# Deferring the shared units of six token tiles in a mixture-of-experts and attention kernel

## What is computed

```python
xn = _layernorm(x)
s = attn(xn)                 # layer norm with gamma, beta; q, k, v; causal softmax; o_proj; + xn
g = silu(ffn(xn))
x = x + s * g

# ffn: E = 8 experts, the 2 best of each token, and a shared part of NS = 2 units
gates = softmax(xf @ router_w.T); topv, topi = top_k(gates, 2)   # then scaled to sum 1
for e in range(8):
    routed += silu(xf @ wg[e]) * (xf @ wu[e]) @ wd[e] * g_e      # D = 512, H = 352
shared = silu(xf @ sg) * (xf @ su) @ sd                          # sg, su: 512 x 704
```

## Time and profile before

| | us |
|---|---|
| three runs | 1258.19, 1260.29, 1260.90 |
| median | 1260.29 |
| the profiled execution | 1259.98 |
| its span in the trace | 1258.2 |
| PE busy | 1176.6 (94%) |
| DVE busy | 598.5 (48%) |
| ACT busy | 456.3 (36%) |
| POOL busy | 343.9 (27%) |

### The profile page before, as it was taken

How to read it: one execution, slowest core, us unless ns; L and a number is a source line. 1 busy time by engine, 2 the same in 40 slices (tenths; PEclk the granted TensorE clock), 3 DMA queues, 4 the chain that set the end, 5 groups by cost and what they waited for, 6 DMA issues and landing times. The chain is left out here.

```text
span 1258.2 us, 21972 instructions
## 1 busy us (share of the span) xinstructions
PE 1176.6 (94%) x6958; PEld 653.6 (52%) x6959; DVE 598.5 (48%) x1198; ACT 456.3 (36%) x822; POOL 343.9 (27%) x430
## 2 busy tenths in 40 slices
PE   5899999999999559999999999997899999999996
PEld 3455555556565235555555555553444444454443
DVE  5555555555555831112112211225765776776455
ACT  4433333333332112222222222223553553554452
POOL 1030000000001431212221221212554564565653
PEclk9899999999999769999999999998999999999999
DMA  8567666766674149977777777765268368257364
GB/s 298 165 161 188 168 165 179 192 166 164 178 187 107 44 92 255 218 188 174 175 183 178 174 179 179 174 153 174 76 151 225 92 149 237 85 123 204 106 146 109
DMA packets 324802, 206.44 MB, mean 164 GB/s; under 512 B 263168, under 2 KB 271368, under 8 KB 324368
## 3 DMA queue, kind: packets, MB, share of 16 engines
q1 hardware_dynamic: 313920, 170.39, 54.1%
q0 software_dynamic: 10800, 35.40, 10.8%
q10 hardware_dynamic: 32, 0.02, 0.0%
HBM read 96.88 MB, written 45.88 MB: 113 GB/s over the span
## 5 line engine op out<-in xcount | busy, mean ns | idle before, releaser
L444 PE MATMUL pair<-arena 128*128 (+1 forms) x3240 | 509.6, 314 | 13.1 <-DMA arena<-arena 13.1
L444 PEld LDWEIGHTS pair<-arena 128*128 128x128 f16 x3240 | 316.2, 98 | 193.0 <-issue 15.0
L451 PE MATMUL bank<-arena 128*128 (+1 forms) x1215 | 289.9, 385 | 8.9 <-ACT arena L884 5.1
L451 PEld LDWEIGHTS bank<-arena 128*128 128x128 f16 x1215 | 119.9, 99 | 138.8 <-issue 13.1
L1265 DVE SCALAR_TENSOR_TENSOR arena<-pair,arena 128x352 f32<-128x352 f32 x71 | 37.2, 525 | 269.9 <-ACT arena L1237 266.1
L1517 PE MATMUL pair<-arena 128*128 128x512 f16 x672 | 154.1, 385 | 2.9 <-PEq L1122 2.9
L1237 ACT ACTIVATE arena<-pair 128x352 f32<-128x352 f32 x71 | 33.0, 464 | 214.5 <-PE pair L444 214.5
L1517 PEld LDWEIGHTS pair<-arena 128*128 128x128 f16 x672 | 66.6, 99 | 78.9 <-issue 7.4
L1545 PE MATMUL bank<-arena 128*128 128x512 f16 x432 | 98.6, 379 | 7.9 <-DMA arena<-arena 7.9
L201 POOL TENSOR_TENSOR root_seed<-var_eps,minus_half 128x1 f32<-128x1 f32 x32 | 17.6, 551 | 318.6 <-DVE var_eps L210 318.5
L1532 PE MATMUL pair<-arena 128*128 128x512 f16 (+3 forms) x576 | 98.9, 326 | 1.1 <-ACT arena L1589 1.1
(11 more groups left out here) (164 smaller groups left out, 1162.0 us busy)
## 6 DMA issues: line engine op xcount, KB each, us to landing
arena<-in_L_attn_x_dram SPq DMA_DIRECT2D x96, 256.0 KB, 3.4
slot_rows<-arena SPq DMA_DIRECT2D x71, 256.0 KB
xn_rows<-arena SPq DMA_DIRECT2D x32, 256.0 KB, 2.4
shared_rows<-arena SPq DMA_DIRECT2D x32, 256.0 KB, 2.6
arena<-shared_rows SPq DMA_DIRECT2D x32, 256.0 KB, 2.9
out_dram<-arena SPq DMA_DIRECT2D x32, 256.0 KB, 3.3
arena<-in_L_ffn_wg_dram SPq DMA_DIRECT2D x32, 176.0 KB, 3.0
arena<-in_L_ffn_wu_dram SPq DMA_DIRECT2D x32, 176.0 KB, 3.4
```

Of the source, the lines that this page charges most:

```text
L444: last = pe.matmul(bank[:, 0:H], xt[:, a, c, :], weights(c, b, col), start=(c == 0 and i == 0), stop=(c == KC - 1 and i == 2))
L451: last = pe.matmul(bank[:, :], ht[:, a, c, :], weights(c, b), start=(start and c == 0 and i == 0), stop=(stop and c == HC - 1 and i == 2))
```

## The change

- **Stage 0.** The x tiles 0 and 1 are loaded behind the second part of `qkv`, ahead of the third part and of `o_proj`. Their statistics are behind group 7, their normalisation behind group 8, their split behind group 13. The four split groups stand ahead of "product 0" of k = 2 and 3, and PE's wait ahead of "product 1" no longer takes these two in. The rest of x (`x_low`) is made by POOL instead of DVE, in stage 1 too.
- **Order of tiles in stage 1.** Tiles 5, 9, 13, 17, 21 and 25 (`DEFERRED`) are routed and stored in their turn, but their shared units come last: steps 0 to 25 take the other 26 tiles (`USUAL`), steps 26 to 31 the deferred ones. In a step whose tile number jumps by two, two tiles are prepared and routed. For a deferred tile SP transposes the rows once more, now from `xn_rows` in DRAM (`turn_late`). Three xt buffers, two banks each for y and for the logits ("two row banks").
- **Expert weights** are loaded and split in steps 0 to 23: the 24 tiles of `wd` one a step, the 32 of `wg`, `wu` over the 18 steps that prepare one tile.
- **Routing** is cut in 11 pieces, one or more per half step, from step 25, b = 0 to step 30, b = 0, each behind `h_low` or `down_low` on DVE. The multiply by the token number is no longer a POOL instruction per group: eight DVE instructions with two scalar operands (128x71) make each group's hot tile.
- **Stages 1 to 3 are one block**, no barrier between them. PE goes from `unit_in(63)`, `unit_down(61)` to slot 0, `unit_down(62)`, slot 1, `unit_down(63)`. SP asks for the transposes of slots 0 and 1 and POOL for their gathers during steps 30 and 31. Stage 1 is written out without a loop.
- **SP's queue** has, per step: the next tiles' transposes, stores and loads, `turn_late`, the h transpose of the half step before, the weight loads, the y store, the h transpose of b = 0.
- Stage 4, make_gates and the slot loop's order are as before, but for names and banks.

```diff
+        DEFERRED = (5, 9, 13, 17, 21, 25)
+        USUAL = [n for n in range(NT) if n not in DEFERRED]
+        LATE = len(USUAL)
...
-                      + [("product", 0, k) for k in range(KC // 2, KC - 1)] + [("split", 0, n) for n in range(KC)]
-                      + [("product", 0, KC - 1)] + [("product", 1, k) for k in range(KC)])
-            X_STATS, X_NORMAL, X_SPLIT = 2 * KC + 1, 3 * KC, 3 * KC + 2
+                      + [("split", 0, n) for n in range(KC)] + [("product", 0, k) for k in range(KC // 2, KC)]
+                      + [("product", 1, k) for k in range(KC)])
+            X_STATS, X_NORMAL, X_SPLIT = 2 * KC - 1, 2 * KC, 3 * KC + 1
...
-                                pe.wait_ge(lo_done, g if m == 0 else g - 1)
+                                pe.wait_ge(lo_done, g if m == 0 else g - KC // 2)
...
-        def keep_x_low(dve, t, u):
-            dve.wait_ge(x16_hi, t + 1)
-            nc.vector.tensor_tensor(x16[u][:, 1], xb[u], x16[u][:, 0], ALU.subtract).then_inc(x16_lo, 1)
+        def x_low(pool, t):
+            u = t % 2
+            pool.wait_ge(x16_hi, t + 1)
+            pool.tensor_tensor(x16[u][:, 1], xb[u], x16[u][:, 0], ALU.subtract).then_inc(x16_lo, 1)
+            pool.wait_ge(x16_lo, t + 1)
...
+            def routed_in(s):
+                return range(USUAL[s] + 1, USUAL[s + 1] + 1) if s + 1 < LATE else ()
+            def normal_in(s):
+                return routed_in(s + 1)
...
+                    def turn_late(s):
+                        d = s - LATE
+                        t = DEFERRED[d]
+                        sp.wait_ge(xn_stored[t % 2], (t // 2 + 1) * 16)
+                        sp.wait_ge(gu_done, 2 * s - 2)
+                        sp.dma_start_transpose(xt[d % 2].rearrange("p s c t -> p (s c) t"), xn_rows[t * P:(t + 1) * P, :]
+                                               ).then_inc(late_turned[d % 2], 16)
...
-                v.tensor_tensor(hot_tile[n % RING], column[:].unsqueeze(1).to_broadcast([P, TG, W]),
-                                slot_hi[:, c, tiles].unsqueeze(2).to_broadcast([P, TG, W]), ALU.is_equal
-                                ).then_inc(in_tile_ready, 1)
+                for i in range(TG):
+                    t = first + i
+                    v.tensor_scalar(hot_tile[n % RING][:, i, :], column[:], slot_hi[:, c, t:t + 1], token_mid[:, t:t + 1],
+                                    ALU.is_equal, ALU.mult).then_inc(hot_ready, 1)
...
+            ROUTING = LATE - 2
+            def routing(dve, s, b):
+                at = 2 * (s - ROUTING) + b - 1
+                if at == 1:
+                    pick_best(dve, 0)
+                elif at == 2:
+                    pick_best(dve, 1)
...
+                elif at == 11:
+                    name_experts(dve)
+                    name_tokens(dve)
+            def hot_products_in(s, b):
+                at = 2 * (s - ROUTING) + b - 1
+                return {7: (0, 1), 8: (2,), 9: (3, 4), 10: (5,), 11: (6, 7)}.get(at, ())
...
+                    router(0)
+                    for s in range(NT):
+                        for b in range(2):
+                            n = 2 * s + b
+                            if n == 2 * ROUTING + 5:
+                                ranks()
+                            if s == 0:
+                                pe.wait_ge(shared_lo, NS if b == 0 else 2 * NS)
+                            unit_in(n, b)
+                            if s > 0:
+                                if n == 2:
+                                    pe.wait_ge(shared_lo, len(splits))
+                                unit_down(n - 2, b)
+                            if b == 1:
+                                for t in routed_in(s):
+                                    router(t)
+                            for m in hot_products_in(s, b):
+                                hot_product(m)
```

More of the change, by code:

```diff
@@ L348, in _ @@
                     seed(pool, 1, 1)
+                    x_low(pool, 0)
+                    x_low(pool, 1)
                 @block.tensor
@@ L1110, in early, with over_slots @@
+            slot_y_stored = slot_rows_stored
             def early(j, n):
                 return isinstance(j, int) and j < n
-            def over_slots(eng, tile, peeled, done=0):
-                for j in range(done, peeled):
-                    tile(j, j % 2, j // 2, False)
-                with eng.Fori(peeled // 2, (T - 1) // 2) as i:
+            def over_slots(eng, tile, first):
+                with eng.Fori(first // 2, (T - 1) // 2) as i:
                     tile(2 * i, 0, i, False)
@@ L1181, in _, with router @@
                 @block.tensor
                 def _(pe):
+                    def router(t):
+                        pe.wait_ge(x_turned[t % 3], (t // 3 + 1) * 16)
+                        wait(pe, logits_kept, t - 1)
+                        for c in range(KC):
+                            for i, (a, b) in enumerate(PARTS):
+                                last = pe.matmul(logit_bank[t % 2][:, 0:E], xt[t % 3][:, a, c, :],
+                                                 rw_split[:, c, b, :],
+                                                 start=(c == 0 and i == 0), stop=(c == KC - 1 and i == 2))
+                        last.then_inc(logits_done, 1)
@@ new lines, in unit_down, with ranks @@
+                    def unit_down(n, b):
+                        t = n // 2
+                        pe.wait_ge(h_turned[b], (t + 1) * 16)
+                        if b == 0:
+                            wait(pe, y_ready, t - 1)
+                        down(pe, ht[b], lambda c, s: shared_down[:, b, c, s, :], y_bank[t % 2],
+                             b == 0, b == 1).then_inc(y_done, 1)
+                    def ranks():
+                        pe.wait_ge(picks_ready, 1)
+                        picked = both16.rearrange("p t e -> p (t e)")
+                        pe.matmul(rank_bank[:, 0:NT * E], before[:, :], picked, start=True, stop=True)
+                        pe.matmul(count_bank[:, 0:NT * E], ones16[:, :], picked, start=True, stop=True
+                                  ).then_inc(ranks_done, 1)
@@ new lines, in hot_product @@
+                    def hot_product(n):
+                        pe.wait_ge(lane_ready, n + 1)
+                        pe.wait_ge(hot_ready, (n + 1) * TG)
+                        for t in range(TG):
+                            last = pe.matmul(token_bank[:, 0:W], hot_lane[n % RING][:, t, :], hot_tile[n % RING][:, t, :],
+                                             start=(n == 0 and t == 0), stop=(n == 2 * PARTS_HOT - 1 and t == TG - 1),
+                                             skip_group_check=True)
+                        last.then_inc(hot_used, 1)
@@ L1240, in slot_tile @@
+                        act.wait_ge(slot_gu_done, j + 1)
+                        if early(j, 2):
+                            act.wait_ge(h_lo, 2 * NT - 1 + j)
+                        else:
+                            wait(act, slot_h_lo, j - 1)
+                        nc.scalar.activation(sbuf[u], g_banks[u][:, 0:H], ACT.Silu,
+                                             scale=UNIT_SCALE).then_inc(slot_silu_done, 1)
+                        slot_h_high(j, u, k)
                         if last:
```

1130 lines of the change are left out of this document (557 added, 573 removed).

## The result

The changed kernel takes **1220.24 us** (median of 4 runs, 1218.99 to 1221.0), the kernel before 1259.47 us in the same comparison (4 runs, 1258.19 to 1260.9). The ratio is 0.9682, with a 95% interval of 0.9664 to 0.9701: faster, by 39 us. The forecast was 1217 us with a range of 1211 to 1228, so sign and range held and the time came out 3.2 us above the forecast. The span of the profiled execution is 1219.3 us where the sum had 1215.0: 4.3 us to explain.

A forecast was written before the change was run, and what follows sets the result against it. PE was taken to bound the kernel, with gains only where its busy share dips. Span 1258.2 - 37.2 - 7.4 + 0.7 + 0.7 = 1215.0 us, giving a forecast of 1217 us, range 1211 to 1228.

The forecast's parts named there:

- Term A: End of stage 1 to slot 3: routing hidden under the deferred units, so PE's waits and slow clock go, -37.2 us.
- both fit: Gather and transpose for slot 0 fit in the about 18 us between naming the tokens and slot 0.
- Term B: Stage 0: PE's wait for DVE's splits and slow matmuls behind it go, -7.4 us, bounds 6.8 and 8.2.
- a bad end: Stage 0 and first steps of stage 1: each x_low on POOL may block DVE by its full 1.3 us.
- Term C: First steps of stage 1: the wait for the down splits stays and may grow, +0.7 us, bounds 0 and +1.3.
- Stage 1's steady part: 0: Middle of stage 1: same PE work, DVE's idle half takes the extra in-splits, so no change in time.
- Term D: Routing pieces on DVE in the late half steps: three PE waits of some 0.2 us, +0.7, bounds 0 and +3.
- rival 3: DVE's pieces too big: two-scalar instructions cost 0.33 not 0.20 us, PE waits three times, 1221 to 1226 us; chance 0.12.
- The end (0): From slot 3 to the kernel's end: forecast gain of 0 us.
- One sign of being right: Start of the kernel: only one slice of low PE digits left, 9s from slice 2 on.
- Rivals 1 and 2: Deferred rows' DRAM transpose delays h transposes in steps 26 to 31: 1231 us at 8 us (0.10); a loss, 1279 (0.03).
- Rival 4: Stage 1 written out: straight code stalls on instruction supply, 0.3 us per in-unit, 1236 us; chance 0.03.

The follow-up runs named there:

- The run without cover: Changed kernel with all 11 routing pieces, ranks, hot products and first slot's transpose behind stage 1's last units: 1264.76 us, ratio 1.0048 to the kernel before.
- the run one step later: Changed kernel with every routing piece one step (two half steps) later, first slot's transpose behind the h transpose of the half step before: 1226.1 us.

## Why the prediction came out as it did

**Term A (-37.2) was right, mechanism and size.** Between in-unit 4 and slot 3 went 33.3 us. The waits that stand there and are no part of A are 3.1 (h transposes) and 0.4 (hot product, 371.58): 33.3 + 3.1 + 0.4 = 36.8. With the 4.0 us that the run with the h transpose in between gave for those four waits, it is 37.7. Slot 0 starts without a wait behind a down-unit, as the sum had assumed. The run without cover gave the waits back one by one. That "both fit" is true with 5.0 us of slack, as the run one step later showed. The slack was smaller than the prediction had it: it put slot 0 about 18 us behind the naming of the tokens, and they lie 13.8 us apart (398.83 to 412.65), with two in-units and three down-units between them and not three and four.

**Term B (-7.4) was right:** 7.0. The working's weak point was the splits. PE's wait, bounded by 0 and 1.4, was 0.92, and the two product groups ahead of it ended 0.4 us later than before (26.52 against 26.11):

```profile
27.45 5.34 PE L391 MATMUL pair<-arena 128*128 128x512 f16 x24 [0.92 <-DVE arena L435]
```

DVE's and POOL's timelines show why:

```profile
23.84 3.46 DVE L435 SCALAR_TENSOR_TENSOR arena<-arena 128x512 f16<-128x512 f32 x4 [0.29 <-ACT arena L414]
```

```profile
22.77 2.78 POOL L252 TENSOR_TENSOR arena<-arena 128x512 f16<-128x512 f32 x2 [5.71 <-ACT arena L247]
```

The four splits took 3.46 us instead of 2.49, with POOL's two rests running until 25.55. That is the sharing which the prediction had named a bad end. By the Trainium skill, SBUF — State Buffer, section SBUF: two separate sides, a DVE instruction with two SBUF inputs is held off for the whole of a GpSimd instruction that reads SBUF and has the lock. The trace agrees that they hold each other up; the price was 1.0 us here, less than the full overlap of 1.7 us.

**Term C (+0.7) had the wrong sign:** 0.9 us were gained. The wait for the down splits did grow as said, from 3.2 to 3.8 us. Not in the sum was the clock (granted 0.72 from 47 to 53 us before, 1.00 from 40 to 50 now): before, the first in-unit there took 5.35 us and the down-unit behind the wait 3.15; now the first two in-units take 7.32 together, and the down-unit 3.80. Slow running cost about 3.2 us before (5.35 - 3.74, 3.15 - 2.11 and 4.24 - 3.74) and 1.7 now. The size is not firm: six of the ten traces of the changed kernel and its variants have this stretch at 23.5 us instead of 24.8, with a slow start (the first two in-units in 9.0 us together), a shorter wait (2.6) and a down-unit at full speed behind it (2.12). By those the gain is 2.1.

**"Stage 1's steady part: 0" is the step that failed first,** by 4.0 us. It looked at busy shares of DVE, POOL and the DMA engines and at the usual step. It did not walk SP's queue through a step with two tiles, although it noted that such steps exist. Six issues stand ahead of the h transpose there, 5.5 us from 192.00 to 197.46, and the slack was less. That makes two of the four waits, 1.9 of 3.1 us; the other two are transposes that landed slowly in steps with one tile. The run with the h transpose in between removed all four and took 4.0 us from the stretch, which is the term's size.

**Term D (+0.7, bounds 0 and 3) held,** but with luck. The instruction with two scalar operands has a duration of 0.307 to 0.329 us, not the 0.20 of the earlier trace rows, and rival 3 had given 1221 to 1226 for 0.33. DVE's timeline shows what the rival had wrong:

```profile
368.49 1.91 DVE L764 TENSOR_SCALAR arena<-column,arena,token_mid 128x71 f16<-128x71 f32 x8
370.29 1.23 DVE L766 TENSOR_TENSOR arena<-lane,arena 128x1024 f16<-128x1024 f32 x1
371.43 0.53 DVE L1270 SCALAR_TENSOR_TENSOR arena<-pair,arena 128x352 f32<-128x352 f32 x1
```

From the first of eight to the instruction behind them are 1.80 us, 0.225 each: their durations overlap. A group is 371.43 - 368.49 = 2.94 us, against 2.8 in the sum and 3.9 in the rival, which had added up durations. DVE is at 8.7 to 9.4 of 10 us in these steps and PE waits once for 0.41.

**The end (0) is the step that failed second,** by 2.4 us. "Stage 3 as before" took over the waits in the slots, and even allowed that they might fall away. The load of the folded weights cost 3.2 us before and 7.7 after, as the runs with the load in pieces show for the stretch from slot 3 to stage 4's first product. That is 4.5 us more at this place; the waits alone say the same (2.7 and 0.5 before, 6.1 and a slow in-unit of 1.5 after). Some of it came back behind it: from the last slot's in-unit to stage 4's first product are 17.35 us (806.95 to 824.30) where there were 19.00 (844.16 to 863.16). All of these 1.7 us are one down-unit that ran in 3.80 us before (852.97, granted clock 0.79 from 850 to 858 us) and runs in 2.12 now (1.00 from 814 to 820); why the clock was down there before was not tested. The two failed steps together are 6.4 us. The span missed by 4.3 only, since C came out 1.6 better than its term, and A and D together 0.8, against 0.4 lost in B: that much of the nearness is luck.

One sign of being right did not come: the second slice was to be at 9 and is at 7. The waits that stage 1 starts with (2.4 at router 0, 3.8 for the down splits) fall into it.

**Rivals 1 and 2 are out.** The transposes out of DRAM land in 3.1, 3.3 and 4.9 us (least, median, most), which is under the 5.7 where the cost would begin, and no down-unit of steps 26 to 31 waits. SP spends 1.23 us to issue one. **Rival 4** is out: PE is busy for 100.00 of 100 us in the straight code once SP's order is mended, as it was in the loop, so neither form was held by its instructions. The Trainium skill, Runtime: NRT & Kernel Launch, section on instruction fetch, has a taken branch break the prefetch if its target isn't already in the fetched window. No gap of PE is to be seen in the loop, so the trace shows no such price; whether the loop's target was in the window it can't show.

## What to carry to other kernels

A chain of small dependent steps at a stage's seam can be hidden whole, if enough independent units are kept back for it; count the slack behind its last link too, since here one step more cost 6 us. Then walk every in-order queue through the rare step, not the usual one. Where a queue issues transfers for two consumers, look at which one is waited for soonest; here the place between the two x transposes beat the one behind both, but with `x_low` on DVE the place ahead of both won nothing. A large load in front of small urgent ones was worth cutting and moving back.

## What the hardware showed beyond that

- The two DMA transposes issued next behind the 2 MB load hold SP for 2.9 to 5.6 us each instead of 1.2 (nine traces), so one large transfer delays the queue itself and not only the data. In the slots with a piece of 256 KB the issues are 1.2 to 1.3 us.
- An instruction's duration in the trace is not its price in a row: eight `tensor_scalar` of 128x71 with two scalar operands show 0.317 us each (median) and come every 0.225.
- A subtraction on POOL stretches one on DVE beside it. All 24 splits of line 1285 take 1.21 to 1.44 us in the changed kernel, where they stand beside `x_low` on POOL, and 0.69 in the run with `x_low` on DVE. One of them, DVE's line first, then POOL's:

```profile
50.45 1.22 DVE L1285 SCALAR_TENSOR_TENSOR arena<-arena 128x512 f16<-128x512 f32 x1 [1.22 <-ACT arena L1183]
```

```profile
49.96 1.16 POOL L252 TENSOR_TENSOR arena<-arena 128x512 f16<-128x512 f32 x1 [3.07 <-ACT arena L247]
```

Even so the move of this work to POOL paid, since at its place on DVE it stood behind other work: 1220 against 1237 us.
